# Recurrent two-layer kernel: the transpose of the maxima behind the last pair of scores, and one filler quarter per head group in a later gap

## The chip, the cores and the metric

The kernel runs on one core of a Trainium2 chip. The metric is the device time of one execution in microseconds (us). Engines: TensorE (PE; its weight loads are PEld), VectorE (DVE), ScalarE (ACT), GpSimd (POOL) and SyncE (SP, DMA issues).

## The reference

Two layers on x of shape (4, 512, 512), float32. Each is `x + s * g` on the layer norm `xn` of x.

- Layer 0, s: attention with 32 query heads and 8 key/value heads of dimension 16, rotary embedding, causal mask: `softmax(q k^T / 4 + mask) v`, then times `wo`. 4 query heads share a key/value head.
- Layer 0, g: a mixture of 8 experts, `silu` of the mean over the top 2 of `relu(xn @ W_e + b_e)`, chosen by `xn @ W_gate + b_gate`.
- Layer 1, s: a long convolution over the channel axis of 512 with a kernel from a state-space model (S4), computed from 64 complex poles, plus `D * u`.
- Layer 1, g: `silu(xn @ W^T + bias)` with a block-scaled weight.

## The kernel before, in words

Three stages follow each other on all engines: stage a (0 to about 101 us of the profile: layer norm, projections, routing), stage b (attention and experts) and stage c (from about 604 us: layer 1). Only stage b is touched.

**Stage b** has 32 head groups: 4 batches (b) times 8 key/value heads (h), each with its 4 query heads. I number them 0 to 31 (8 b + h). Each group is computed twice over. First in rows: ten score products S1 (`scores_1`, line 1562), whose masked maxima VectorE takes (`maxima`, line 1374). Then transposed: ten score products S2 (`scores_2`, lines 1588 and 1591), in which the negated row maximum enters as two more rows of the stacked operand, so that ScalarE can take the exponentials directly (`exps`, line 1485). GpSimd zeroes the masked part of the diagonal blocks (`select`, line 1308), and TensorE multiplies with the values (`values`, line 1615) in the order of key blocks 0, then 2, 3, 1.

How the maxima get there: VectorE splits them into two float32r parts (`maxima_parts`, lines 1387 and 1389), TensorE transposes them, the **turn** (`turn_maxima`, line 1599), VectorE copies the rows out (`maxima_rows`, line 1397), and SP and ACT send each one half into the operand by DMA (line 1291). ACT's DMA issue stands ahead of its last two exponentials of the group.

The stages of three groups are interleaved. While TensorE runs S2 of group g, it runs S1 of g+1, and at the end S1 products 0 and 1 of g+2. S1 has three PSUM banks: product n waits until maxima n-3 are taken; S2 likewise for the exponentials. The turn of g+1 uses the bank of S1 product 2 of g+2.

**Fillers.** Between the blocks of scores TensorE has five gaps, 0 to 4, in which it works on units of four **quarters**. A quarter is one 128x128 by 128x512 float32 product: of an expert tile (x, line 1643; the first of a unit has a bias product, line 1641) or of the output projection of a token tile (o, line 1654). `PLAN` orders the units, `SIZES` says how many quarters each gap of each group takes: SIX and EIGHT alternate, with SIX in the even groups 2 to 24, 26, 27 and 28 and EIGHT in the odd groups 3 to 25 and 29. I call these even and odd groups. All units use bank 7, so a unit's first quarter waits until ACT has read the last one (line 1495 for an expert tile).

**What follows from SIZES.** An expert tile's rows are gathered from HBM by four indirect DMAs of GpSimd (`gather`, line 1321), then transposed by VectorE (`expert_x`, line 1438), then used. `turns()` and `gathers()` compute from the gaps at which units begin and end where VectorE's transposes stand (slot 0: between the parts and the copy of the maxima; slot 1: behind the group's end) and in which of GpSimd's three slots per group the gathers stand: slot 0 behind the select of block 0, slot 1 behind that of block 2, slot 2, the last, behind those of 3 and 1. At most three gathers fit into a slot. A gather of tile m waits for the transpose of tile m-2.

At a group's end VectorE reads the values out of PSUM by a transpose (`rows_of`, line 1407: the **read**), normalises them (1412, 1416), in odd groups transposes a pair (1424), and goes on with maxima 2 to 9 of the next group. All orders are written out by hand; counts of semaphores tie the engines together.

Of the kernel before, what the change touches and what calls it, by code (L numbers as in the profile page):

```python
# [46 lines left out]
ORDER = [0, 2, 3, 1]  # L47
GAPS = 5
PLAN = "x" * 12 + ("ooxoo" + "x" * 9) * 2 + "ooxoo" + "x" * 6
SIX, EIGHT = (2, 1, 1, 1, 1), (2, 2, 1, 1, 2)  # L50
NONE = (0,) * GAPS
SIZES = [NONE, (0, 0, 0, 2, 2)] + [SIX, EIGHT] * 12 + [SIX, SIX] + [SIX, EIGHT, (2, 2, 1, 1, 0), NONE]
QUARTERS = [SIZES[KV * b:KV * (b + 1)] for b in range(NB)]
# [164 lines left out]
def build(nc, x_d, wq_d, wk_d, wv_d, wo_d, wg_d, bg_d, we_d, be_d, lam_d, p_d, q_d, vct_d, ct_d, bp_d, dd_d,  # L218
          step_d, wft_d, sc_d, bf_d, const_d, dft_d, out_d):
    ctx = ExitStack()  # L220
    with ctx:
# [532 lines left out]
        def pe_taps(e, c):  # L754

            t = nc.tensor
            if c == 0:
                e.wait_ge(s4_roots, 1)
                e.wait_ge(c_dft, 16 * 2 * KB)
                e.wait_ge(b_m, NB * NG * NJ)  # L760
            for k in range(KB):
                i = t.matmul(bank[5], roots[:, c, k:k + 1].to_broadcast([P, P]), dft[c][:, k, :],
                             start=(c + k == 0), stop=(c + k == KB))
            if c == 1:
                i.then_inc(s4_taps, 1)
# [468 lines left out]
        def next_group(b, h, n):  # L1234

            return b + (h + n) // NG, (h + n) % NG
# [382 lines left out]
        def pe_b(e):  # L1619
# [51 lines left out]
            def go(b):  # L1671
                for h in range(1 if b == 0 else 0, NG):
                    following = next_group(b, h, 1) if b * NG + h + 1 < NB * NG else None
                    after = next_group(b, h, 2) if b * NG + h + 2 < NB * NG else None
                    scores(e, (2, 3, 4), following, (0, 1, 2), (b, h))
                    quarters(b, h, 0)
                    scores(e, (5, 6, 7), following, (3, 4, 5), (b, h))
                    quarters(b, h, 1)
                    if (b, h) == (NB - 1, NG - 1):
                        pe_taps(e, 0)  # L1680
                    scores(e, (8, 9), following, (6, 7), (b, h))
                    values(e, b, h, 0)
                    quarters(b, h, 2)
                    if (b, h) == (NB - 1, NG - 1):
                        pe_taps(e, 1)
                    if following:
                        turn_maxima(e, *following)
                    scores(e, (0, 1), after, (8, 9), (b, h))
                    quarters(b, h, 3)
                    for j in ORDER[1:]:  # L1690
                        values(e, b, h, j)
                    quarters(b, h, 4)
# [461 lines left out]
```

## Time and profile before

| | us |
|---|---|
| runs | 708.52, 708.9, 706.66; median 708.52 |
| profiled execution | 706.16, span 704.4 |
| TensorE busy | 646.2 (92%) |
| VectorE busy | 560.6 (80%) |
| GpSimd, ScalarE busy | 351.3, 292.9 |
| granted TensorE clock, mean | 0.96 |
| chain that ended last | TensorE 45%, VectorE 38%, issue 7%, unknown 6% |

The profile is of one execution. The span runs from the first instruction to the last. Busy time of TensorE is modelled at the ends of matmuls. The chain goes back and forth between TensorE and VectorE, so neither alone explains the time; the waits and the timeline of single groups tell more.

### The profile page before, as it was taken

Reading aid. Unit: us, or ns where it says so; the run is one execution under the profiler, and the core shown is the slowest. Engines: PE = TensorE matmul, PEld = TensorE weight load, DVE = VectorE, ACT = ScalarE, POOL = GpSimd, SP = SyncE. Lnnn points to the kernel's source line nnn. Section 1 sums busy time; section 2 is a strip of 40 time slices with the busy share of each in tenths; the row PEclk is TensorE's granted clock in tenths of the full one; section 3 lists DMA queues with packets and bytes.
Section 4 is the critical chain, followed back from the end, with each engine's and each line's share of the span. In section 5 each row is a group of like instructions: output and inputs, shape, how many; then the busy total and the mean of one; then the engine's idle time right before and its main releaser. Section 6 shows DMA issues by size and latency. Waiting matters only on the chain.

```text
span 704.4 us, 12346 instructions
## 1 busy us (share of the span) xinstructions
PE 646.2 (92%) x3560; PEld 346.5 (49%) x3560; DVE 560.6 (80%) x1789; ACT 292.9 (42%) x535; POOL 351.3 (50%) x497
## 2 busy tenths in 40 slices
PE   8999997897899899988989999998999899999997
PEld 4888774333333334433333433343433343478886
DVE  5698998777777778887767888777987887769995
ACT  5353316333334344443434444443444443444442
POOL 3777621645454633366453346636325434656630
PEclk9999998588889999999999999999999999999999
DMA  7599979274647363372725517364353525658751
GB/s 254 153 335 277 321 181 175 45 119 137 117 138 137 85 115 56 56 121 73 118 61 96 81 34 129 85 103 86 72 105 74 144 79 208 139 113 224 197 143 74
DMA packets 55567, 92.67 MB, mean 132 GB/s; under 512 B 10328, under 2 KB 23320, under 8 KB 55504
## 3 DMA queue, kind: packets, MB, share of 16 engines
q1 hardware_dynamic: 41890, 66.45, 40.3%
q0 software_dynamic: 8576, 18.62, 12.3%
q10 hardware_dynamic: 5038, 6.84, 3.8%
q8 instruction: 29, 0.48, 0.3%
q14 instruction: 34, 0.28, 0.2%
HBM read 61.93 MB, written 29.43 MB: 130 GB/s over the span
## 4 chain that ended last, share of the span: by engine, by line
PE 45%; DVE 38%; issue 7%; another core or an unknown queue 6%; POOL 3%; DMA 1%; ACT 0%; SPq 0%; DVEq 0%; POOLq 0%; ACTq 0%
DVE bank L1374 18%; PE bank L1643 8%; PE bank L991 8%; PE bank L1562 6%; PE bank L2071 6%; PE bank L2076 4%; PE bank L1615 4%; DVE arena L1374 3%; PE bank L1654 3%; DVE arena L1438 2%; DVE arena L1407 2%; DVE m_parts L1387 2%; PE bank L1588 1%; PE bank L969 1%
## 5 line engine op out<-in xcount | busy, mean ns | idle before, releaser
L1485 ACT ACTIVATE arena<-bank 128x512 f32<-128x512 f32 x320 | 175.2, 598 | 215.3 <-PE bank L1588 159.8
L1374 DVE CUSTOM_DVE_ANT_0 bank<-bank,cst 128x384 f32<-128x384 f32 (+3 forms) x512 | 233.7, 523 | 28.0 <-PE bank L1562 21.4
L1321 POOL DMA_INDIRECT arena<-xn_rows,slots_i x156 | 148.6, 953 | 64.6 <-issue 34.0
L1308 POOL TENSOR_SCALAR_AFFINE_SELECT arena<-arena 128x512 f32<-128x512 f32 x128 | 81.9, 653 | 185.0 <-ACT arena L1485 181.3
L1643 PE MATMUL bank<-w_e,arena 128*128 x312 | 165.7, 638 | 0.0
L1562 PE MATMUL bank<-kt,qt 48*128 48x512 f32 (+1 forms) x496 | 123.9, 360 | 21.3 <-DVE arena L1374 17.7
L1562 PEld LDWEIGHTS bank<-kt,qt 48*128 48x128 f32 x496 | 77.1, 198 | 110.7 <-DVE arena L1374 65.8
L1588 PE MATMUL bank<-qt,kt 50*128 50x512 f32 x256 | 100.8, 477 | 0.9 <-ACT arena L1485 0.9
L1615 PE MATMUL bank<-arena 128*32 128x512 f32 (+3 forms) x1024 | 88.8, 462 | 0.6 <-ACT arena L1485 0.4
L1643 PEld LDWEIGHTS bank<-w_e,arena 128*128 128x128 f32 x312 | 55.0, 196 | 60.5 <-issue 56.9
L1374 DVE DVE_READ_ACCUMULATOR2_ANT arena<- 128x1 f32 x512 | 72.6, 142 | 0.0
L1407 DVE STREAM_TRANSPOSE arena<-bank 128x512 f32<-128x512 f32 x32 | 22.9, 717 | 54.9 <-remote 41.3
L1654 PE MATMUL bank<-w_proj,arena 128*128 128x512 f32 x128 | 65.0, 622 | 0.0
L825 POOL TENSOR_TENSOR s_tok<-arena 128x256 f32<-128x256 f32 (+1 forms) x64 | 33.5, 557 | 25.8 <-DVE arena L541 20.4
L991 PE MATMUL bank<-proj_high,xh 128*128 128x264 f32 (+1 forms) x128 | 45.9, 359 | 0.2 <-DVE xl L522 0.2
L1588 PEld LDWEIGHTS bank<-qt,kt 50*128 50x128 f32 x256 | 43.7, 192 | 4.4 <-ACT arena L1485 2.4
L1495 ACT ACTIVATE arena<-bank 128x512 f32<-128x512 f32 x39 | 23.4, 599 | 53.1 <-PE bank L1643 48.3
L1615 PEld LDWEIGHTS bank<-arena 128*32 128x32 f32 x1024 | 25.2, 112 | 37.5 <-issue 25.0
L991 PE MATMUL bank<-proj_low,xh 128*128 128x264 f32 (+1 forms) x128 | 43.5, 340 | 0.0
L991 PE MATMUL bank<-proj_high,xl 128*128 128x264 f32 (+1 forms) x128 | 43.2, 338 | 0.0
L1654 PEld LDWEIGHTS bank<-w_proj,arena 128*128 128x128 f32 x128 | 21.2, 189 | 26.6 <-issue 24.0
L537 DVE TENSOR_TENSOR arena<-bank,cst 128x128 f32<-128x128 f32 (+1 forms) x63 | 27.2, 476 | 6.2 <-PE bank L991 5.9
(168 smaller groups left out, 958.0 us busy)
## 6 DMA issues: line engine op xcount, KB each, us to landing
qt<-turned_parts SPq DMA_DIRECT2D x96, 128.0 KB
turned_parts<-qk_parts SPq DMA_DIRECT2D x8, 1280.0 KB
expert_rows<-arena SPq DMA_DIRECT2D x39, 256.0 KB
w_e<-in_L_ffn_W_e ACTq DMA_DIRECT2D x24, 256.0 KB, 6.2
kt<-turned_parts SPq DMA_DIRECT2D x96, 64.0 KB, 6.0
arena<-in_L_attn_x SPq DMA_DIRECT2D x16, 256.0 KB, 6.2
xn_rows<-arena SPq DMA_DIRECT2D x16, 256.0 KB, 6.0
w_e<-in_L_attn_x SPq DMA_DIRECT2D x16, 256.0 KB
```

The costliest lines, as they stand in the source:

```text
L991: i = t.matmul(out[u % 2][:, 0:n], x[:, u % 2, k, :], w[part][:, k, :], start=(k == 0 and x is xh and part == 0), stop=(k == KB - 1 and pa ...
L1308: g.affine_select(out=diag, in_=diag, compare_op=ALU.is_ge, fill=0.0, base=0, pattern=[[0, 2], [0, HALF], [1, P]], channel_multiplier=-1). ...
L1321: e.indirect_dma_start(xg[m % 2][:, n * P:(n + 1) * P], None, xn_q, bass.IndirectOffsetOnAxis(ap=slots_i[:, n, m:m + 1], axis=0)).then_inc ...
L1374: i = v.tensor_tensor_reduce(out=part, in0=part, in1=const("mask")[:, S - w:], scale=1.0, scalar=LOWEST, op0=ALU.add, op1=ALU.max, accum_o ...
L1407: v.transpose(oe.rearrange("p q c -> p (q c)"), bank[4]).then_inc(b_o, 1)
L1485: nc.scalar.activation(pt[:, s, first:second + 1:second - first].rearrange("p c r q -> p c (r q)"), s2_bank(b, h, n).rearrange("p (c x) -> ...
L1562: i = t.matmul(s1_bank(b, h, n)[:, at:at + w], stack[rows, x if r is None else r, q * P:w], kt[rows, h // 2 % 2, h % 2, 0:w], start=(x == ...
L1588: i = t.matmul(to, keys(j), queries[:, q:q + 2], start=True, stop=True)
L1615: i = nc.tensor.matmul(bank[4][VW * r:VW * (r + 1), j * P:], vb[:, j, h, :], pt[:, r // HALF, at:at + TPB - j, r % HALF, :], start=(j == O ...
L1643: i = t.matmul(bank[7], xgt[:, m % 2, k * P:(k + 1) * P], w_e[:, ex[m], k, :], start=False, stop=(k == KB - 1))
L1654: i = t.matmul(bank[to], ot[:, (b * PAIRS + k) % (PAIRS + 1), u, :], wo[:, k, :], start=(k == 0), stop=(k == KB - 1))
L2071: i = t.matmul(bank[2 + u % 2][:, :], x[:, u % 2, k, :], (w_high, w_low)[part][:, k, :], start=(k + n == 0), stop=(k + n == KB + 1))
```

## The change

It has two parts, and the schedules that are computed from `SIZES` follow.

```
-SIX, EIGHT = (2, 1, 1, 1, 1), (2, 2, 1, 1, 2)
+SIX, EIGHT = (1, 1, 1, 1, 2), (2, 1, 1, 2, 2)
```
```
                     quarters(b, h, 2)
                     if (b, h) == (NB - 1, NG - 1):
                         pe_taps(e, 1)
+                    scores(e, (0, 1), after, (8, 9), (b, h))
                     if following:
                         turn_maxima(e, *following)
-                    scores(e, (0, 1), after, (8, 9), (b, h))
                     quarters(b, h, 3)
```

TensorE's queue around the turn in group 14 (an even group), before. L1599 is the turn, L1562 and L1588 are the score products, L1641 and L1643 filler quarters, L1615 the values; b_mx is the count of VectorE's maxima parts.

```order
L1643 MATMUL bank<-w_e,arena 128x512
L1599 MATMUL bank<-cst,m_parts 32x128 [waits b_mx]
L1562 MATMUL bank<-kt,qt 128x512 [waits b_m,b_ld0]
L1588 MATMUL bank<-qt,kt 128x512 [waits b_e]
L1562 MATMUL bank<-kt,qt 128x512 [waits b_m]
L1588 MATMUL bank<-qt,kt 128x512 [waits b_e]
L1641 ISA [waits m_ye]
L1641 MATMUL bank<-be,sel_e 128x512
L1643 ISA [waits m_xt]
L1643 MATMUL bank<-w_e,arena 128x512
L1615 MATMUL bank<-arena 32x256 [waits b_sel,b_e]
```

The same place in the changed program:

```order
L1562 MATMUL bank<-kt,qt 128x512 [waits b_m,b_ld0]
L1588 MATMUL bank<-qt,kt 128x512 [waits b_e]
L1562 MATMUL bank<-kt,qt 128x512 [waits b_m]
L1588 MATMUL bank<-qt,kt 128x512 [waits b_e]
L1599 MATMUL bank<-cst,m_parts 32x128 [waits b_mx]
L1643 ISA
L1643 MATMUL bank<-w_e,arena 128x512
L1615 MATMUL bank<-arena 32x256 [waits b_sel,b_e]
L1615 MATMUL bank<-arena 32x256 x3
L1615 MATMUL bank<-arena 32x128 [waits b_sel,b_e]
```

The turn stands behind the four score products, which then no longer wait with it, and ahead of gap 3's quarter. The quarters of the units shift by one, so that another quarter of tile 18 stands there.

TensorE's queue in group 13 (an odd group), from the third S1 product of the second block to the first of the third block, that is gap 1, before:

```order
L1562 MATMUL bank<-kt,qt 128x384 [waits b_m]
L1562 MATMUL bank<-kt,qt 128x128
L1588 MATMUL bank<-qt,kt 128x512 [waits b_e]
L1643 ISA
L1643 MATMUL bank<-w_e,arena 128x512
L1624 TENSOR_LOAD eid_i
L1624 ISA x2
L1643 ISA
L1643 MATMUL bank<-w_e,arena 128x512
L1562 MATMUL bank<-kt,qt 128x256 [waits b_m]
```

And in the changed program:

```order
L1562 MATMUL bank<-kt,qt 128x384 [waits b_m]
L1562 MATMUL bank<-kt,qt 128x128
L1588 MATMUL bank<-qt,kt 128x512 [waits b_e]
L1643 ISA
L1643 MATMUL bank<-w_e,arena 128x512
L1624 TENSOR_LOAD eid_i
L1624 ISA x2
L1562 MATMUL bank<-kt,qt 128x256 [waits b_m]
```

One L1643 of gap 1 is gone from ahead of S1 product 8; it stands in gap 3, behind the turn.

GpSimd's queue in groups 8 to 11, before. L1301 begins batch 1 (group 8), each L1308 is a select (four to a group), each L1321 a gather.

```order
L1301 COPY arena<-v_tok 128x32x16
L1308 AFFINE_SELECT arena<-arena 128x2x256
L1321 DMA arena<-xn_rows,slots_i 128x128
L1308 AFFINE_SELECT arena<-arena 128x2x256 x4
L1321 DMA arena<-xn_rows,slots_i 128x128 x3
L1308 AFFINE_SELECT arena<-arena 128x2x256
L1321 DMA arena<-xn_rows,slots_i 128x128
L1308 AFFINE_SELECT arena<-arena 128x2x256 x7
L1321 DMA arena<-xn_rows,slots_i 128x128 x3
```

And in the changed program:

```order
L1301 COPY arena<-v_tok 128x32x16
L1308 AFFINE_SELECT arena<-arena 128x2x256
L1321 DMA arena<-xn_rows,slots_i 128x128
L1308 AFFINE_SELECT arena<-arena 128x2x256 x7
L1321 DMA arena<-xn_rows,slots_i 128x128 x3
L1308 AFFINE_SELECT arena<-arena 128x2x256
L1321 DMA arena<-xn_rows,slots_i 128x128
L1308 AFFINE_SELECT arena<-arena 128x2x256 x4
L1321 DMA arena<-xn_rows,slots_i 128x128 x3
```

The three gathers of tile 14 stand behind the first select of group 9 before, and behind its last one after: seven selects on are the four of group 9 with three of group 8. The same happens in groups 17 and 25. Beside this VectorE's transposes (line 1438) of tiles 12, 22, 32 go from the end of groups 8, 16, 24 to slot 0 of the group behind, those of tiles 7, 17, 27 from the end of groups 4, 12, 20 to slot 0 of 5, 13, 21, and those of tiles 8, 18, 28 from slot 0 of 5, 13, 21 to the end of these groups. ACT's and SP's reads and stores of finished units move with the gap in which the unit ends.

## Rows read from the trace of the kernel before

**Rows 1.** The page, busy time of the engines.
```profile
PE 646.2 (92%) x3560; PEld 346.5 (49%) x3560; DVE 560.6 (80%) x1789; ACT 292.9 (42%) x535; POOL 351.3 (50%) x497
```
**Rows 2.** Busy time by stretch: all groups, group 13. Columns: stretch, length, engines, clock.
```profile
134.87:573.50 438.63, 398.94 (x2197) 166.48 (x2196) 347.82 (x1258) 185.07 (x339) 217.05 (x269) 0.96 0.48 95
323.58:339.66 16.08, 14.21 (x76) 5.79 (x78) 12.28 (x43) 6.61 (x12) 10.11 (x12) 1.00 0.36 89
```
**Rows 3.** Waits: who, for whom, us in total, times, longest.
```profile
DVE arena L1407 <- remote: 41.3, 16, 3.0
...
DVE bank L1374 <- PE bank L1562: 21.4, 31, 3.2
...
PE bank L1599 <- DVE m_parts L1389: 14.7, 27, 1.6
```
**Rows 4.** Timeline of group 13: start, us, engine, line, what, idle before.
```profile
330.33 0.94 POOL L1321 DMA_INDIRECT arena<-xn_rows,slots_i  x1 [0.17 <-issue]
...
330.73 0.43 DVE L1374 CUSTOM_DVE_ANT_0 bank<-bank,cst 128x256 f32<-128x256 f32 x1 [0.65 <-PE bank L1562]
...
332.54 1.24 POOL L1308 TENSOR_SCALAR_AFFINE_SELECT arena<-arena 128x512 f32<-128x512 f32 x2
332.61 1.21 DVE L1389 SCALAR_TENSOR_TENSOR m_parts<-arena,m_parts 128x16 fp32r<-128x16 f32 x1
333.74 0.70 DVE L1438 STREAM_TRANSPOSE arena<-arena 128x512 f32<-128x512 f32 x1
...
333.88 0.28 PE L1599 MATMUL bank<-cst,m_parts 128*32 128x128 f32 x1 [0.76 <-DVE m_parts L1389]
...
335.19 0.95 POOL L1321 DMA_INDIRECT arena<-xn_rows,slots_i  x1 [1.41 <-DVE arena L1438]
...
335.37 1.08 ACT L1485 ACTIVATE arena<-bank 128x512 f32<-128x512 f32 x2 [3.03 <-PE bank L1588]
...
335.82 1.53 PE L1615 MATMUL bank<-arena 128*32 128x256 f32 x24
...
337.29 1.98 PE L1643 MATMUL bank<-w_e,arena 128*128 x4
...
337.69 0.94 POOL L1321 DMA_INDIRECT arena<-xn_rows,slots_i  x1 [0.30 <-issue]
...
339.66 0.72 DVE L1407 STREAM_TRANSPOSE arena<-bank 128x512 f32<-128x512 f32 x1 [2.78 <-remote]
```
**Rows 5.** Timeline of group 14, from the turn to the read.
```profile
348.57 0.28 PE L1599 MATMUL bank<-cst,m_parts 128*32 128x128 f32 x1 [0.31 <-DVE m_parts L1389]
...
348.79 0.72 PE L1588 MATMUL bank<-qt,kt 50*128 50x512 f32 x2
...
350.64 1.50 PE L1615 MATMUL bank<-arena 128*32 128x256 f32 x24
...
352.39 0.95 POOL L1321 DMA_INDIRECT arena<-xn_rows,slots_i  x1 [0.30 <-issue]
...
354.37 0.72 DVE L1407 STREAM_TRANSPOSE arena<-bank 128x512 f32<-128x512 f32 x1 [2.77 <-remote]
```
**Rows 6.** Timeline of groups 17 and 18: values, reads and turn.
```profile
396.29 1.50 PE L1615 MATMUL bank<-arena 128*32 128x256 f32 x24
...
397.86 0.72 DVE L1407 STREAM_TRANSPOSE arena<-bank 128x512 f32<-128x512 f32 x1 [1.25 <-PE bank L1615]
...
407.80 0.28 PE L1599 MATMUL bank<-cst,m_parts 128*32 128x128 f32 x1 [0.52 <-DVE m_parts L1389]
...
409.74 1.50 PE L1615 MATMUL bank<-arena 128*32 128x256 f32 x24
```
**Rows 7.** Timeline of TensorE's stops, and a stretch of group 15 as in rows 2.
```profile
311.39 0.44 PE L1562 MATMUL bank<-kt,qt 48*128 48x384 f32 x1 [0.99 <-DVE arena L1374]
...
357.22 0.44 PE L1562 MATMUL bank<-kt,qt 48*128 48x384 f32 x1 [1.20 <-DVE arena L1374]
...
358.54:361.95 3.41, 3.32 (x7) 1.83 (x8) 2.33 (x13) 1.08 (x2) 2.74 (x4) 0.50 0.22 58
```
**Rows 8.** Groups of instructions: line, engine, operation, count, busy, mean ns.
```profile
L1389 DVE SCALAR_TENSOR_TENSOR m_parts<-arena,m_parts 128x16 fp32r<-128x16 f32 x32 | 12.7, 398 | 1.1
```

More of the change, by code:

```diff
@@ L1685, in go @@
                         pe_taps(e, 1)
+                    scores(e, (0, 1), after, (8, 9), (b, h))
                     if following:
                         turn_maxima(e, *following)
-                    scores(e, (0, 1), after, (8, 9), (b, h))
                     quarters(b, h, 3)
```

## The prediction

> **What bounds the kernel now.** I read the page first [rows 1]: TensorE is busy 92% of the span, VectorE 80%. Then the stretch of the head groups, 134.9 to 573.5 us [rows 2]: TensorE is busy 399 of 439 us, VectorE 348. So 40 us of TensorE's time is idle there, and the question is whose waits make it. Then the table of waits [rows 3]: TensorE waits 14.7 us in 27 places for VectorE's negated maxima before the turn (line 1599), and VectorE waits 41.3 us in 16 places before it reads the values out of PSUM (line 1407), with the releaser "remote", which is none that the trace can name.
>
> The timeline of group 13 shows what that is [rows 4]. The last values end at 335.82 + 1.53 = 337.35, but VectorE starts to read them at 339.66, 2.3 us late. In between GpSimd issues three gathers, 1.25 apart, the last from 337.69 to 338.63, and VectorE goes on 1.0 behind its end. Group 14 repeats it [rows 5]: values end 352.14, the last gather ends 353.34, the read starts 354.37. Where no gather stands there the read follows at once: values end 397.79, read 397.86 [rows 6]. I take it that TensorE's counts reach the others late while gathers are issued. All 16 "remote" places have three gathers in GpSimd's last slot of the group, and of the groups in steady running that have them only 20 and 21 escape.
>
> So there are two kinds of cycle. **Held groups**: the turn, VectorE's transpose of an expert tile (0.70), three gathers, one microsecond, the read: 339.66 - 333.88 = 5.78, and 5.80 in group 14, whatever TensorE does between; then VectorE's own chain from the read to the next turn, 348.57 - 339.66 = 8.91 in group 14, 16.08 - 5.78 = 10.30 in group 13 [rows 2, 4, 5]. VectorE and GpSimd bound them. **Free groups**: values end 3.44 behind the turn, and the chain from read to turn takes 9.94 [rows 6]; TensorE and VectorE are nearly level.
>
> **The change part by part.**
>
> *The turn behind the last score pair.* The four score products take 0.72 [rows 5]. They now fill TensorE's wait, at most 14.7 in 27 places, mean 0.54. But the turn starts when line 1389 ends (333.82, turn 333.88), before and after: nothing on VectorE becomes earlier. What follows it (the copy of the rows, two DMA issues, the last two exponentials) ends at 336.45, 2.57 behind the turn [rows 4], and the last values need it. Today the values start 1.94 behind the turn; in an even group they could start 0.7 sooner, but their last part still waits for the exponentials, so their end stays. Value 0 of a possible 0 to -14.7; I take 0, since the row nearest, the exponentials' end, doesn't move. On TensorE's queue the scores, the quarters and the values stand behind the turn's wait as before, the one score pair no longer. The new place also moves the turn behind the wait for the next stacks' loads; these were issued more than a group (14 us) earlier, so I add nothing.
>
> *The quarter out of gap 1 in odd groups.* A quarter costs 0.96 (two take 1.98 with the last one's tail [rows 4]). In group 13 VectorE stands 0.65 before 330.73, waiting for the scores behind the two quarters. With one quarter these come 0.96 earlier and the wait is gone. Eight odd groups (3, 5, 7, 13, 15, 21, 23, 29) have it at 0.65 to 0.9: 8 x 0.7 = -5.6. Bounds: 0, if the counts are then held by the gather at 330.33, and -7. In even groups the quarter leaves gap 0, where VectorE doesn't wait if the read was held: 0. Group 2: -0.5.
>
> *The quarters added behind.* In odd groups one more in gap 3 makes the values start at +2.1 instead of +1.94; held groups don't feel it. In free odd groups (9, 11, 17, 19, 25) TensorE reaches the turn later by the scores' 0.72 less its present wait (0.2 to 0.76): +0.3 each, and the same in 27 and 30: +2.1. Bounds 0 and +5.
>
> *Expert tiles and gathers that move along.* The schedule derives them. Three transposes (0.70) leave VectorE's chain from read to turn in groups 5, 13, 21 and three enter it in 6, 14, 22: 0 within 0.3. In 9, 17, 25 the gathers of tiles 14, 24, 34 move from the group's head to its last slot. These groups are free now and become held: the cycle of the group behind goes from 13.45 (411.24 - 397.79, values to values [rows 6]) to 14.79 (352.14 - 337.35 [rows 4, 5]): 3 x 1.3 = +3.9, bounds 0 and +4.2.
>
> *The stall of line 1389.* In group 13 it takes 1.21 and ends with the two selects that started before it (332.54, 1.24 together [rows 4]); its mean over 32 is 0.40 [rows 8]. The selects here stand behind two gathers (the first at 330.33), so they don't move up, while VectorE arrives 0.7 earlier and can pass before them. In 5, 13 and 21 fewer gathers are ahead, the selects move too, and part of the stall stays. Over seven held odd groups I take 7 x -0.3 = -2.1. Bounds: -0.8 x 4 for the four with a full stall (1.21 down to the mean) and +0.8 x 3 for those without, if they get one.
> The Trainium skill (SBUF — State Buffer, section "Who interferes with whom") states that a VectorE instruction with two SBUF inputs and a GpSimd instruction that reads SBUF exclude each other, whoever issues first holding for its whole length. The 1.21 beside the 1.24 agrees. By that rule passing or not passing a select is all or nothing, and the term would be -3 or +2 rather than between.
>
> *Clock.* In group 15 TensorE stood 1.20 before 357.22; from 358.54 to 361.95 the granted clock is 0.50, 1.2 GHz [rows 7], which takes 1.7 of its time. The mean clock of 0.96 over 438.6 [rows 2] is 17.5 us of it, 6 in the first 12 us, the rest in groups 3, 4, 15, 20 and 21; I reckon that 8 of it is on the path. Odd groups lose this stop (a quarter more stands ahead of it). Even groups reach their second block of scores 0.96 earlier, less 0.2 for the later values, and wait there for the maxima: group 12's stop, 0.99 before 311.39 [rows 7], becomes 1.75, others 1.2 to 1.6. I take -1, bounds -5 and +6.
> The Trainium skill (TensorE: Matmul & The Clock Gate, Part 1) says that the throttled clock is the default and activity releases it. That speaks against the change, which gathers idle time into fewer, longer stops. The trace agrees in one place, 1.20 and then 0.50.
>
> **Sum.** -5.6 - 0.5 + 2.1 + 0 + 3.9 - 2.1 - 1.0 = -3.2. The profiled execution took 706.16 (span 704.4 and 1.8 around it); it would be 703.0. The median of the runs shown is 708.52, 2.4 above it, so against the median the forecast is 705.3; I say 705.2. A measurement of this kernel can tell about 0.3%, 2.1 us, from no change: below 706.4 is faster, above 710.6 slower.
>
> **Rivals.**
> *Nothing is left of it* (0.22). The 5.78 of the held groups doesn't move; if the scores' counts are held by the gather in gap 1 too, -5.6 halves and the stall stays: about 708.5. For it: the gather at 330.33 lies right there. Against it: VectorE's wait at 330.73 ended while that gather ran.
> *Clock: slower* (0.18). Thirteen even groups run behind a held read once 9, 17 and 25 are held too. If the stop at their second block lets the clock fall each time, the half-speed stretch (3.41) adds 1.7 of TensorE's work, of which VectorE's slack covers 0.6: 13 x 1.1 = 14.3 instead of the 7 left in the sum. That is +7 on the forecast: 712.3. It decides from about six such falls on. For it: group 15 did it at 1.20. Against it: group 12's 0.99 passed without.
> *TensorE is the bound after all* (0.12). Then the 14.7 comes off whole, less the +3.9 and +2.1 that remain and a few us for gaps whose quarter was needed: about -10, 698.5. For it: 92% busy. Against it: 5.78 and 5.80 in rows 4 and 5, with two quarters behind the values in one and one in the other.
> *The forecast* (0.48), own range 702 to 708.
>
> **Range and chances.** 700.5 to 711 leaves out the far half of the TensorE rival and the bad end of the clock one. Faster: three quarters of the forecast's 0.48, the TensorE rival's 0.12, 0.03 of the first rival: 0.51. Slower: 0.17 from the clock and 0.03 from the rest: 0.20. Same: 0.29.
>
> **What would show it.** The turn's wait (14.7) is small, but "remote" waits before line 1407 stand in 19 places instead of 16, with groups 9, 17 and 25 among them and reads 5.8 behind the turn there. VectorE's waits for line 1562 fall from 21.4 to about 14. The chain from read to turn is 8.2 to 9.5 in groups 13 and 15. The clock is below 1 in some even groups' second block; if it falls in more than six, I am on the wrong side. If reads no longer follow the gathers' end by 1.0, the picture of the held counts is wrong.

## The result, and the profile after

| | before | after |
|---|---|---|
| median of 7 runs, us | 708.9 (706.66 to 710.03) | 715.62 (711.6 to 720.61) |
| ratio, 95% interval | | 1.0103 (1.0071 to 1.0135) |
| profiled execution, us | 706.16, span 704.4 | 720.61, span 718.8 |
| granted clock, mean of that execution | 0.960 | 0.940 |

The change costs 1%. The forecast was 705.2 with a range up to 711, so it has the wrong sign. The profiled execution is the longest of its seven, so its sums are somewhat large; where that matters I use a second trace, or the clock and span of every run.

The page of the kernel after, busy times and granted clock in 40 slices:

```profile
PE 655.7 (91%) x3560; PEld 348.2 (48%) x3560; DVE 553.6 (77%) x1789; ACT 290.9 (40%) x535; POOL 352.6 (49%) x497
PEclk9999997589899999989999899989989998999999
```

Against [rows 1], TensorE is busy 9.5 us longer with the same instructions: the clock row has an 8 every few slices. Its waits (engine, line, releaser: us in total, times, longest), to be held against [rows 3]:

```profile
DVE arena L1407 <- remote: 44.1, 16, 3.8
DVE arena L1397 <- PE bank L1599: 22.5, 19, 3.3
DVE bank L1374 <- PE bank L1562: 16.9, 25, 1.3
PE bank L1615 <- ACT arena L1485: 14.0, 18, 2.2
PE bank L1599 <- DVE m_parts L1389: 2.1, 2, 1.4
```

TensorE's wait before the turn is gone (14.7, now 2.1), as forecast, and so is part of VectorE's wait for scores (21.4, now 16.9). In their place VectorE waits 22.5 us for the turn (4.5 before, a row that I had not looked at), and TensorE waits 14.0 for the last exponentials before the last values (0.4 before). Group 16 (the turn at 380.34) shows both:

```profile
378.12 1.13 PE L1654 MATMUL bank<-w_proj,arena 128*128 128x512 f32 x2
378.96 0.55 DVE L1389 SCALAR_TENSOR_TENSOR m_parts<-arena,m_parts 128x16 fp32r<-128x16 f32 x1
379.68 0.50 PE L1562 MATMUL bank<-kt,qt 48*128 48x512 f32 x1 [0.43 <-DMA qt<-turned_parts]
380.34 0.28 PE L1599 MATMUL bank<-cst,m_parts 128*32 128x128 f32 x1
380.66 0.28 DVE L1397 COPY arena<-bank 32x128 f32<-32x128 f32 x1 [1.15 <-PE bank L1599]
381.41 0.86 PE L1615 MATMUL bank<-arena 128*32 128x256 f32 x16
382.83 0.85 PE L1615 MATMUL bank<-arena 128*32 128x384 f32 x8 [0.56 <-ACT arena L1485]
```

Line 1389 ends at 379.51, TensorE's filler at 379.25. In the old order the turn would have started at about 379.57, since it follows line 1389 by 0.06 there. Now the first score product waits 0.43 for the load of its stack, the four products take 0.66, and the turn starts 0.83 behind line 1389. The values then start 1.07 behind the turn (1.94 before) and stop 0.56 for the exponentials, which hang on the turn as before.

Group 17, one of the three that were to become held:

```profile
396.29 1.50 PE L1615 MATMUL bank<-arena 128*32 128x256 f32 x24
397.49 0.95 POOL L1321 DMA_INDIRECT arena<-xn_rows,slots_i  x1 [0.30 <-issue]
399.50 0.72 DVE L1407 STREAM_TRANSPOSE arena<-bank 128x512 f32<-128x512 f32 x1 [3.79 <-remote]
```

Values end 397.79, the last gather 398.44, the read starts 1.06 later, 5.75 behind the turn. That step held.

The clock, in the group that follows (TensorE's rows, then the stretch's clock: us, busy times, PEclk):

```profile
402.41 0.44 PE L1562 MATMUL bank<-kt,qt 48*128 48x384 f32 x1 [0.76 <-DVE arena L1374]
404.54 2.07 PE L1654 MATMUL bank<-w_proj,arena 128*128 128x512 f32 x2
```
```profile
403.87:410.69 6.82, 6.82 (x23) 2.57 (x23) 4.63 (x22) 2.04 (x4) 1.87 (x3) 0.50 0.48 81
```

TensorE stops 0.76 before the second block, and from 403.87 to 410.69 it has 0.50, 1.2 GHz; two quarters take 2.07 instead of 1.13. Such stretches between 148 and 600 us sum to 27.3 us in the first trace of before (17.1 and 20.5 in two later ones) and 47.8 in that of after; in a second trace of after (below) to 41.0. There eight of them lie in even groups, 8, 10, 12, 16, 18, 20, 24 and 28, and each of the eight stands behind a stop of 0.80 to 1.87 us before the second block of its group; two stops as long before a filler, 1.86 and 1.90 us in groups 6 and 14 of the same trace, have none behind them. Three of the eight:

```profile
254.54:257.95 3.41, 3.41 (x14) 1.42 (x18) 2.47 (x15) 1.94 (x4) 0.64 (x1) 0.50 0.93 151
285.26:288.67 3.41, 3.41 (x18) 1.21 (x17) 3.13 (x16) 1.08 (x2) 1.63 (x3) 0.50 0.58 117
...
558.33:561.74 3.41, 3.41 (x14) 1.42 (x18) 2.46 (x15) 1.34 (x3) 0.64 (x1) 0.50 0.98 203
```

### The profile page after: what moved, and what is told of

Same layout as the page of the kernel before. It is cut to its first block, busy times and chain, and to the rows that moved or that the text cites. A ratio compares the mean times of both kernels' runs of the same rounds, so it can differ in the third digit from the quotient of the medians.

```text
span 718.8 us, 12346 instructions
## 1 busy us (share of the span) xinstructions
PE 655.7 (91%) x3560; PEld 348.2 (48%) x3560; DVE 553.6 (77%) x1789; ACT 290.9 (40%) x535; POOL 352.6 (49%) x497
## 4 chain that ended last, share of the span: by engine, by line
PE 53%; DVE 23%; issue 7%; another core or an unknown queue 5%; DMA 4%; POOL 3%; ACT 2%; SPq 1%; ACTq 1%; DVEq 0%; POOLq 0%
DVE bank L1374 9%; PE bank L1643 9%; PE bank L1562 7%; PE bank L991 7%; PE bank L1615 6%; PE bank L2071 5%; PE bank L1654 5%; PE bank L2076 4%; PE bank L1588 2%; DMA arena<-xn_rows,slots_i 2%; DVE arena L1374 1%; ACT arena L1485 1%; DVE arena L1407 1%; POOL w_e L1840 1%
## 5 line engine op out<-in xcount | busy, mean ns | idle before, releaser
L1374 DVE CUSTOM_DVE_ANT_0 bank<-bank,cst 128x384 f32<-128x384 f32 (+3 forms) x512 | 233.0, 521 | 22.0 <-PE bank L1562 16.9
L1308 POOL TENSOR_SCALAR_AFFINE_SELECT arena<-arena 128x512 f32<-128x512 f32 x128 | 83.6, 666 | 201.7 <-ACT arena L1485 198.6
L1321 POOL DMA_INDIRECT arena<-xn_rows,slots_i x156 | 148.9, 955 | 61.1 <-issue 33.6
L1643 PE MATMUL bank<-w_e,arena 128*128 x312 | 165.8, 639 | 5.1 <-DVE arena L1438 4.6
L1562 PE MATMUL bank<-kt,qt 48*128 48x512 f32 (+1 forms) x496 | 125.7, 367 | 20.3 <-DVE arena L1374 17.6
L1562 PEld LDWEIGHTS bank<-kt,qt 48*128 48x128 f32 x496 | 78.9, 205 | 131.9 <-DVE arena L1374 74.5
L1615 PE MATMUL bank<-arena 128*32 128x512 f32 (+3 forms) x1024 | 95.5, 476 | 16.2 <-ACT arena L1485 14.0
L1588 PE MATMUL bank<-qt,kt 50*128 50x512 f32 x256 | 100.3, 479 | 0.9 <-ACT arena L1485 0.9
L1643 PEld LDWEIGHTS bank<-w_e,arena 128*128 128x128 f32 x312 | 54.9, 197 | 57.8 <-issue 53.9
L1654 PE MATMUL bank<-w_proj,arena 128*128 128x512 f32 x128 | 67.5, 641 | 0.9 <-ACT s_tok L1476 0.9
L1615 PEld LDWEIGHTS bank<-arena 128*32 128x32 f32 x1024 | 24.5, 112 | 56.5 <-issue 24.9
L1588 PEld LDWEIGHTS bank<-qt,kt 50*128 50x128 f32 x256 | 44.2, 194 | 5.0 <-ACT arena L1485 2.4
L825 POOL TENSOR_TENSOR s_tok<-arena 128x256 f32<-128x256 f32 (+1 forms) x64 | 33.5, 556 | 25.9 <-DVE arena L541 20.5
L991 PE MATMUL bank<-proj_high,xl 128*128 128x264 f32 (+1 forms) x128 | 43.2, 338 | 0.0
L1654 PEld LDWEIGHTS bank<-w_proj,arena 128*128 128x128 f32 x128 | 21.9, 197 | 29.6 <-issue 23.9
L537 DVE TENSOR_TENSOR arena<-bank,cst 128x128 f32<-128x128 f32 (+1 forms) x63 | 27.3, 476 | 6.3 <-PE bank L991 6.0
```

Of the source, the lines that this page charges most:

```text
L825: i = g.tensor_tensor(o[:, :, :, c, :], xc[:, :, :, c, :], xs[:, :, :, 1 - c, :], op)
L991: i = t.matmul(out[u % 2][:, 0:n], x[:, u % 2, k, :], w[part][:, k, :], start=(k == 0 and x is xh and part == 0), stop=(k == KB - 1 and pa ...
L1308: g.affine_select(out=diag, in_=diag, compare_op=ALU.is_ge, fill=0.0, base=0, pattern=[[0, 2], [0, HALF], [1, P]], channel_multiplier=-1). ...
L1321: e.indirect_dma_start(xg[m % 2][:, n * P:(n + 1) * P], None, xn_q, bass.IndirectOffsetOnAxis(ap=slots_i[:, n, m:m + 1], axis=0)).then_inc ...
L1374: i = v.tensor_tensor_reduce(out=part, in0=part, in1=const("mask")[:, S - w:], scale=1.0, scalar=LOWEST, op0=ALU.add, op1=ALU.max, accum_o ...
L1562: i = t.matmul(s1_bank(b, h, n)[:, at:at + w], stack[rows, x if r is None else r, q * P:w], kt[rows, h // 2 % 2, h % 2, 0:w], start=(x == ...
```

## The experiments

They ran in five sets, each on a chip of its own with runs of before beside them. The chips turned out to be of two kinds (in these sets no chip served twice, so it isn't shown that the chip and not the session makes the difference). On the first kind before takes 704 to 707 us (708.9 on the chip of the record) and VectorE's reads are held, as in the prediction. On the second before takes 670 and no read is held. I call them **held chips** and **free chips**.

Two sums serve for reading. Of each run, the **clock loss** is its span times (1 - granted clock), and the **rest** is the span without it. The 13 runs of after on two held chips scatter around a line of 0.93 us of span for 1 us of clock loss (correlation 0.88), so most of it is on the path. Of each trace, the periods of groups 3 to 29 (values' end to values' end) are split at four points: **lag** (values' end to read), **chain** (read to the end of line 1389), **late** (from there to the turn), **values** (turn to values' end).

| run | change against before | chip | median | ratio (95%) | clock loss | rest |
|---|---|---|---|---|---|---|
| c1_after | all | held | 717.38 | 1.0206 (1.0164 to 1.0248) | +14.5 | -0.9 |
| f1_order | turn behind the pair | held | 711.55 | 1.0121 (1.0084 to 1.0158) | +3.5 | +3.4 |
| f2_sizes | new SIX and EIGHT | held | 706.99 | 1.0047 (1.0022 to 1.0072) | +4.1 | -0.4 |
| g1_odd | new EIGHT | held | 703.7 | 0.9958 (0.9937 to 0.9979) | +2.1 | -5.3 |
| e5_split | turn between S2 and S1 pair | held | 707.24 | 1.0029 (1.0001 to 1.0057) | +2.0 | +0.4 |
| e6_order_loads | turn behind the pair, loads on ACT | held | 719.22 | 1.0208 (1.0176 to 1.024) | +8.5 | +5.5 |
| f3_gathers2 | two gathers in last slot | held | 695.07 | 0.9886 (0.9852 to 0.992) | -2.0 | -6.9 |
| g2_odd_gathers2 | new EIGHT, two gathers in last slot | held | 700.45 | 0.9913 (0.988 to 0.9946) | +0.5 | -7.8 |
| e1, d1 | turn behind the pair | free | 679.72, 681.2 | 1.0138, 1.0144 | +0.5, -0.2 | +8.7, +10.1 |
| e2, d2 | new SIX and EIGHT | free | 680.32, 681.05 | 1.0156, 1.0151 | +2.4, +0.9 | +7.6, +9.2 |
| e3_order_odd | turn behind the pair, new EIGHT | free | 676.17 | 1.0099 (1.006 to 1.0139) | +2.5 | +3.8 |
| e4_odd | new EIGHT | free | 675.66 | 1.0077 (1.0045 to 1.0109) | +1.9 | +3.4 |
| e7_fill | all, a quarter twice | free | 686.93 | 1.0256 (1.0209 to 1.0303) | -0.6 | +17.6 |
| e8_gathers2 | two gathers in last slot | free | 678.91 | 1.0116 (1.0074 to 1.0159) | +1.2 | +6.3 |

The last two columns are differences of means, with 95% intervals of about 1.4 to 2.9 us either way for the clock loss and 1.1 to 2.8 for the rest. The intervals of the doubled ratios are 1.0094 to 1.0183, 1.0092 to 1.0196, 1.0119 to 1.0194 and 1.0109 to 1.0194.

Sums of one trace each, groups 3 to 29, us:

| trace | periods | lag | chain | late | values |
|---|---|---|---|---|---|
| before, mean of three (held) | 406.5 | 42.3 | 267.2 | 1.8 | 95.2 |
| after, mean of two (held) | 418.1 | 35.1 | 261.9 | 17.9 | 103.3 |
| f1_order | 404.6 | 37.6 | 264.0 | 12.2 | 90.9 |
| f2_sizes | 414.7 | 37.4 | 258.2 | 6.1 | 113.1 |
| g1_odd | 402.8 | 38.4 | 255.8 | 2.0 | 106.4 |
| e5_split | 408.8 | 43.7 | 266.4 | 7.1 | 91.6 |
| f3_gathers2 | 391.3 | 14.2 | 262.3 | 1.6 | 113.3 |
| e1_order (free) | 381.1 | 5.3 | 265.2 | 19.0 | 91.4 |

The traces of f1 and f2 are of their shortest and longest execution (705.39 and 713.25), 6 off the medians on either side; I take from them where time stands, and how much from the medians. The three traces of before differ by up to 6 us in the chain (264.3 to 270.2), so smaller differences there say little.

The late term has two sources, which the traces tell apart: the filler in front of the score products can itself end behind line 1389, or the products, 0.60 us from the filler's end to the turn, push the turn. In f1_order fillers that end late make up 1.4 us of the 12.2 and waits for loads 0.5; the rest, about 10, is the products. In the two traces of after late fillers make up 7.4 and 5.9 us, most of it in groups with a half-speed stretch; there too some 10 us are left for the products.

**First set, a free chip.** The parts one by one:

```
e1: the new order, SIX, EIGHT = (2, 1, 1, 1, 1), (2, 2, 1, 1, 2)
e2: the old order, SIX, EIGHT = (1, 1, 1, 1, 2), (2, 1, 1, 2, 2)
e3: the new order, SIX, EIGHT = (2, 1, 1, 1, 1), (2, 1, 1, 2, 2)
e4: the old order, SIX, EIGHT = (2, 1, 1, 1, 1), (2, 1, 1, 2, 2)
```

> The new place of the turn alone, old SIZES. Median of before 708.9, of the changed kernel 715.6. Theory CLOCK (the quarter that leaves gap 0 of the even groups makes TensorE stop before the second block, the clock falls to 1.2 GHz there, and the half-speed stretches cost the 7 us): the stops stay as in before, at most 7 half-speed stretches in stage b, 706 to 709. Rival TURN LATE (the four score products stand ahead of the turn, which starts 0.4 to 0.8 behind line 1389's end in some twelve even groups and in the odd ones too, and all that follows moves): 713 to 716, with no more half-speed stretches than before. Rival HELD READS (groups 9, 17, 25 and the moved transposes): no effect here, within 0.3% of before.

> The new SIZES alone, turn in its old place. CLOCK: stops before the second block in the even groups and half-speed stretches as in the changed kernel (about 54 us of them in stage b against 27 before), 713 to 716. TURN LATE: the turn is not late, 703 to 707. HELD READS: about +4 on before, 712 to 714, with reads held in 9, 17 and 25 and half-speed stretches as before.

> The new place of the turn and the odd groups' new EIGHT; the even groups keep SIX of before, with two quarters in gap 0. CLOCK: the stops before the second block stay under 1.2, few half-speed stretches, odd groups shorter, 703 to 707. TURN LATE: 711 to 715. HELD READS: 711 to 713.

> The odd groups' new EIGHT alone: turn in its old place, SIX of before. CLOCK: 702 to 706, faster than before, since only the odd groups' wait at the third block goes. TURN LATE: the same, 702 to 706. HELD READS: 710 to 713, since this kernel has the gathers of tiles 14, 24 and 34 in the last slot of 9, 17 and 25 too.

Each part alone costs time here, and mostly not by the clock, as the rest shows. In e1 the turn is late by 19.0 us in sum. In e2 and e4 it isn't (1.8 and 1.5), but the values take 117.6 and 116.0 us against 91.4 in e1, with another quarter ahead of them in the odd groups. One wait of e1 and one place (group 16):

```profile
PE bank L1562 <- DMA qt<-turned_parts: 8.0, 10, 2.2
```
```profile
360.22 0.17 DVE L1389 SCALAR_TENSOR_TENSOR m_parts<-arena,m_parts 128x16 fp32r<-128x16 f32 x1
361.16 0.50 PE L1562 MATMUL bank<-kt,qt 48*128 48x512 f32 x1 [1.23 <-DMA qt<-turned_parts]
361.82 0.28 PE L1599 MATMUL bank<-cst,m_parts 128*32 128x128 f32 x1
```

The turn stands behind a product that waits for a DMA, and is 1.43 late. I had added nothing for this wait. No read is held. In e1's group 14 all three gathers of the last slot are issued, the last until 337.02, and VectorE reads at 336.84, 0.13 behind the values (335.86 + 0.85); there is no remote wait in the trace:

```profile
335.86 0.85 PE L1615 MATMUL bank<-arena 128*32 128x384 f32 x8 [0.35 <-ACT arena L1485]
336.08 0.94 POOL L1321 DMA_INDIRECT arena<-xn_rows,slots_i  x1 [0.30 <-issue]
336.84 0.72 DVE L1407 STREAM_TRANSPOSE arena<-bank 128x512 f32<-128x512 f32 x1 [0.82 <-PE bank L1615]
```

**Second set, a held chip.** Before and after again, and two orders:

> The kernel before once more, unchanged: its trace on the chip of this call. In the four kernels run so far on another chip (before 669.99 there, not 708) VectorE's read follows the values at once, though GpSimd issues the same three gathers. If the held reads belong to the chip (theory), the trace has no remote waits before line 1407 and all groups take 13.4 to 14.6 where before takes about 670, and has the 41 us of them where before takes about 708. If they came from the changed orders (rival), this trace has them in either case.

c0_before: 704.43, ratio 0.9999 (0.9971 to 1.0026), 43.2 us of remote waits in 16 places. The held reads are not of the changed orders: the unchanged kernel has them here.

> The changed kernel once more, unchanged, beside before on the same chip. Where before takes about 670: theory TURN LATE adds to e1 (ratio 1.0138) and e2 (1.0156) for 1.025 or more if the two parts cost in different places, and about 1.015 if both push the same wait. Where before takes about 708: 1.010 as measured first.

1.0206: larger than the first 1.0103, with intervals that don't meet. Both say slower; what sets the difference between the chips is open. Here all of the loss is clock loss, 40.0 us a run against 25.5, and the rest is 0.9 less than that of before. On the chip of the record after has 37.8 a run; of before only the profiled execution's clock is known, 28.2, so there it is about +10.

```
e5:
+                    scores(e, (), None, (8, 9), (b, h))
                     if following:
                         turn_maxima(e, *following)
-                    scores(e, (0, 1), after, (8, 9), (b, h))
+                    scores(e, (0, 1), after, (), None)
```

> Old SIZES. The S2 pair (8, 9) goes ahead of the turn, the S1 pair (0, 1) stays behind it. Theory LOADS (in e1 TensorE waits in 10 places, 8.0 us, before S1 product 0 for the DMA of the stacks, which now delays the turn behind it): e1's loss mostly goes, ratio 0.997 to 1.005, and the turn starts within 0.1 of line 1389's end. Rival WORK AHEAD (what delays the turn is the 0.72 of products itself, TensorE being full): half of it stays, ratio 1.006 to 1.010.

1.0029. With the S1 pair behind the turn, three quarters of the order's loss (1.0121 on another held chip, below) are gone. That is in LOADS' range, but its mechanism doesn't stand behind it on a held chip: TensorE waits only 0.5 us for loads before S1 products in f1, and the turn here is still 7.1 us late in sum (12.2 in f1), not within 0.1 each time. With half of the products ahead of the turn about half of the added lateness is left, as WORK AHEAD said, though less than half of the lost time.

```
e6 (on e1):
-                        load_stacks(e, *next_group(b, h, 3))
+                        load_stacks(e, *next_group(b, h, 3), (0,))
 and at the end of ACT's odd groups:
+                        load_stacks(e, *next_group(b, h, 3), (1,))
```

> The new place of the turn with old SIZES (as e1), and ACT issues half of each stack load (six of the twelve DMAs) at the end of the odd groups, so that the load lands some 3 us earlier. LOADS: the waits of line 1562 for the DMA into qt go (8.0 us in 10 places in e1) and the ratio falls from e1's 1.0138 to 1.000 to 1.004. WORK AHEAD: 1.008 to 1.014.

The waits for the load are gone, but the kernel is as slow as after. ACT's copy of a finished unit (line 1495) now stands behind the six issues, and TensorE waits for it (line 1645 is 1643 here):

```profile
371.64 0.60 ACT L1495 ACTIVATE arena<-bank 128x512 f32<-128x512 f32 x1 [2.53 <-issue]
372.61 3.58 PE L1645 MATMUL bank<-w_e,arena 128*128 x4 [2.59 <-ACT arena L1495]
```

The edit has brought a stop of its own (9.0 us in 5 places), so the time tells nothing between the two theories. The trace does: without a wait for loads the turn is still late by 10.4 us in sum.

**Third set, a free chip.** d1 and d2 are e1 and e2 again:

> The new place of the turn alone, old SIZES (the kernel of e1), for a chip on which the reads are held (before about 705). There c1_after lost 2.06% (14.5 us) and its half-speed stretches inside the head groups went from about 5 to 11. WORK AHEAD (the S1 pair ahead of the turn makes the turn and all behind it later by up to 0.72): in held groups VectorE's maxima decide and TensorE has time, so ratio 1.000 to 1.005. CLOCK (the values start at +1.07 behind the turn, stop for the last exponentials, the cycle gets a second stop, and the clock falls): 1.008 to 1.015, with more than 8 half-speed stretches in the groups.

> The new SIZES alone (the kernel of e2) on a chip with held reads. CLOCK by the quarter missing in gap 0 of even groups: stops of 1.2 to 1.9 before the second block, 9 or more half-speed stretches, ratio 1.008 to 1.015. HELD READS in groups 9, 17 and 25 alone: 3 x 1.0 to 1.7 = +3 to +5, less the 4 to 6 of the odd groups' shorter chains: 0.997 to 1.002 and about as many half-speed stretches as before.

They repeat the first set, and say nothing of a held chip.

```
e7 (on after), for the even groups' gap 0 (the same for quarters of the output projection):
+                if twice:
+                    t.matmul(bank[7], xgt[:, m % 2, k * P:(k + 1) * P], w_e[:, ex[m], k, :], start=False, stop=False)
```

> The changed kernel, with the one quarter of gap 0 of the even groups (2 to 24, 26 to 28) computed twice: 16 more quarters, 15 us more work for TensorE, placed where it stood still before the second block; its outputs are not the reference's. CLOCK: the stop before the second block goes and with it most half-speed stretches there; ratio 1.003 to 1.010 against the 1.0206 of c1_after. Rival TENSORE IS THE BOUND: the 15 us come on top, 1.03 to 1.04. If the stops matter but not the clock: 1.018 to 1.022.

1.0256. The edit adds a quarter in 15 groups (the expectation counted 16). No after ran beside it, and on a free chip the clock loss is that of before anyway (-0.6). The clock was not tested.

> The kernel before, but at most two gathers in GpSimd's last slot of a group; the third moves to the first slot of the next group. Theory HELD BY GATHERS (VectorE's read follows the end of the last gather of the slot by 1.0): the last gather ends 1.25 earlier, so the reads of 16 groups follow their values by 1.0 to 1.2 instead of 2.3, and VectorE's remote waits fall from 41 to about 20; 8 to 18 us faster, ratio 0.975 to 0.989. Rival BURST ELSEWHERE (the gather that moves holds the counts at the next group's head as well, where VectorE waits for S1 products): 0.995 to 1.005. On a chip without held reads: 0.997 to 1.003.

1.0116, above the 1.003 expected: where nothing is held, moving a gather only costs. What it costs by was not looked into.

**Fourth set, a held chip.** The parts again (f1 is the kernel of e1, f2 that of e2), and the gathers (f3 is the kernel of e8):

> The kernel before, unchanged, for its trace on this chip. If before takes about 670 here, as on two chips so far, the trace has no remote waits before line 1407, groups 9 to 29 take 13.4 to 13.8 each in pairs of 27.2, and GpSimd's gathers stand and last as on the other chips: then the held reads are of the chip. If about 705, remote waits of 40 to 44 us in 14 to 17 places as in c0_before.

704.04, ratio 1.0002 (0.9973 to 1.003), 44.8 us of remote waits in 17 places.

> The new place of the turn alone, with old SIZES, on the next chip. Twice 1.014 where before takes 670 (10 us in 30 groups, the even groups' turn 0.5 to 1.4 behind line 1389's end). Where before takes 705: WORK AHEAD gives 1.000 to 1.005, since in a held group only VectorE's chain counts; CLOCK gives 1.008 to 1.015 with more than 8 half-speed stretches in the groups.

1.0121, half clock loss (+3.5) and half rest (+3.4). The turn is late by 12.2 us in sum, of which about 10 are the products. Group 15 shows one place without any wait:

```profile
361.97 1.13 PE L1643 MATMUL bank<-w_e,arena 128*128 x2
362.71 0.17 DVE L1389 SCALAR_TENSOR_TENSOR m_parts<-arena,m_parts 128x16 fp32r<-128x16 f32 x1
363.02 0.49 PE L1562 MATMUL bank<-kt,qt 48*128 48x512 f32 x1
363.70 0.28 PE L1599 MATMUL bank<-cst,m_parts 128*32 128x128 f32 x1
```

Line 1389 ends at 362.88, the filler at 363.10, and the turn starts 0.60 behind the filler, 0.82 behind line 1389. So WORK AHEAD has the mechanism, but as I had bounded it (1.005) it is too small, and CLOCK's more than eight stretches are not there either (six, 23.9 us, in its shortest execution).

> The new SIZES alone on the next chip. Twice 1.015 where before takes 670 (odd groups 14.0 to 14.7 instead of about 13.7, because in the free running the quarter moved into gap 3 stands ahead of the values). Where before takes 705: CLOCK by gap 0 gives 1.008 to 1.015 and 9 or more half-speed stretches; held reads in 9, 17 and 25 alone give 0.997 to 1.002.

1.0047: between the two theories, clock loss +4.1 and the rest -0.4. So separately the parts add 3.5 and 4.1 of clock loss, together 14.5 on another held chip and about 10 on the chip of the record. The ratios themselves do about add up: 1.0121 and 1.0047 give 1.0168, between the 1.0103 and the 1.0206 of after. One place where the traces differ in the stops alone is 360 to 425 us, groups 15 to 19. There f2 has one stop of TensorE of over 0.55 us (0.80), f1 has four of 0.56, and neither has a half-speed stretch. In after there are both kinds (1.21, 0.56, 0.76, 0.56), and behind the 0.76 the clock falls. First f2, then f1, then after:

```profile
360.00:425.00 65.00, 60.57 (x353) 25.59 (x360) 52.75 (x203) 29.51 (x54) 28.85 (x38) 1.00 0.41 73
```
```profile
360.00:425.00 65.00, 60.55 (x354) 24.76 (x357) 51.08 (x192) 28.12 (x52) 28.10 (x36) 1.00 0.43 74
```
```profile
360.00:425.00 65.00, 60.49 (x329) 24.71 (x328) 49.06 (x191) 27.05 (x51) 25.76 (x34) 0.95 0.39 67
```

The 0.56 are the new stop before the last values, which the order brings. The 1.21 and 0.76 of after are those before the second block, where the quarter of gap 0 is missing; f2, which misses it too, has none there in this stretch, and its 0.80 stands before the turn. It is one stretch of one trace each: that the two kinds of stop together make the clock fall is suggested by it, not shown.

```
f3:
-            at[(*divmod(g, KV), slot)], waiting = waiting[:3], waiting[3:]
+            n = 2 if slot == 2 else 3
+            at[(*divmod(g, KV), slot)], waiting = waiting[:n], waiting[n:]
```

> The kernel before with at most two gathers in GpSimd's last slot. 1.0116 where before takes 670 and no read is held. Where before takes 705: HELD BY GATHERS gives reads 1.0 to 1.2 behind the values instead of 2.3, remote waits of about 20 instead of 41 us, and 0.975 to 0.995 (the 8 us that it costs on the other chips taken off the gain); BURST ELSEWHERE gives 1.005 to 1.015 with as many us of remote waits as before.

0.9886, faster than both kernels. The lag falls from 42.3 to 14.2 us, as HELD BY GATHERS said. But the values' part grows by 18 (95.2 to 113.3), and the remote waits of f3 tell where it went (its lines are one higher: 1398 is the copy of the turned maxima, 1408 the read, 1486 the exponentials):

```profile
DVE arena L1398 <- remote: 16.2, 10, 2.1
ACT arena L1486 <- remote: 12.7, 7, 3.5
DVE arena L1408 <- remote: 2.1, 1, 2.1
```

Group 15 shows one:

```profile
356.10 0.28 PE L1600 MATMUL bank<-cst,m_parts 128*32 128x128 f32 x1
356.14 0.94 POOL L1322 DMA_INDIRECT arena<-xn_rows,slots_i  x1 [0.31 <-ACT arena L1486]
358.20 0.28 DVE L1398 COPY arena<-bank 32x128 f32<-32x128 f32 x1 [1.54 <-remote]
```

The moved gather now stands beside the turn, and the copy goes on 1.12 behind its end (357.08). So other counts of TensorE's can be held by a gather too, not only that of the values. Not every one is: in [rows 4] VectorE went on at 330.73, in the middle of the gather of 330.33. Both theories were partly right.

**Fifth set, a held chip.** g1 is the kernel of e4, and g2 has the edit of f3 besides.

> The odd groups' new EIGHT alone (the kernel of e4, 1.0077 where before takes 670), turn and SIX as before. Where before takes 705: if the loss of the new SIZES (f2, 1.0047, 37 us of half-speed stretches in the groups against 17 to 27 before) comes from the quarter missing in gap 0 of the even groups (CLOCK), this one has the stretches of before and is 0.988 to 0.997, since the chain from read to maxima parts gets 8 to 9 us shorter over groups 3 to 29 and the three newly held groups give back 4. If it comes from EIGHT itself (values later behind the two quarters of gap 3, three more held reads), 1.001 to 1.006.

0.9958, 3.0 us faster than before; the rest is 5.3 less. The forecast for the odd groups' terms was -3.8 (-5.6 + 3.9 - 2.1), so their total is about right. By the trace that is in part luck: the chain is 11.4 shorter against the 7.7 forecast, lag and values together 7.3 longer against 3.9. With f2's 1.0047 the new SIX costs about 0.9% (two chips); on the free chip of the first set e2 and e4 differ by 0.8% as well. Most of it is not clock: the rests differ by 4.9 and 4.2 us, the clock losses by 2.0 and 0.5. Where in the groups it arises was not followed further.

> The same with at most two gathers in GpSimd's last slot. Where before takes 705: f3 gave 0.9886 for the two gathers alone; with EIGHT, under CLOCK 0.978 to 0.986, under EIGHT ITSELF 0.988 to 0.994, the best kernel of the study in either case if the two gains add. Where before takes 670: 1.012 to 1.020.

0.9913: no better than f3 (0.9886, on another chip). The gains don't add. The values' part is 125.5 us in its trace against 95.2 of before, and ScalarE's exponentials alone have 21.4 us of remote waits in 12 places.

## Why the prediction was wrong, point by point

- **The turn, value 0, "the turn starts when line 1389 ends, before and after".** This is the step that failed most. It was true of before, where the sum of the late term is 1.8 us. In f1, the order alone, it is 12.2, about 10 of it by the four products; in after it is 17.9, with late fillers beside that. The row that I read it from (turn 0.06 behind line 1389) was one where TensorE was waiting 0.76; group 14 beside it had 0.31 [rows 5]. The mean wait was 0.54, and the products that I moved ahead of the turn take 0.60 of queue time. In the three traces of before the filler ends 0.6 or more ahead of line 1389 in only 7, 3 and 3 of 27 groups. An estimate from these traces, 0.60 less the head start of each group, gives 7, 9 and 10 us of lateness, near what f1 showed. I had priced it at +2.1, in the free odd groups (and 27 and 30) only; 11 and 19, which I named among these, are not free, their reads follow the turn by 5.8. The order alone measured 1.0121, about +8.5.
- **"The new place also moves the turn behind the wait for the next stacks' loads; ... I add nothing."** Failed too. The last of the twelve loads is issued some 7 us ahead, not 14 (group 16: its last ones begin at 372.15 and 372.61, the wait ends at 379.68). On a free chip that wait is 8.0 us of the 19.0 by which the turn is late. On held chips it is small (0.4 in after, 0.5 in f1), and the products decide.
- **"Their end stays" for the values.** Right for the order: 3.34 behind the turn in group 16. What I didn't draw from it is that the 0.87 by which the values start sooner becomes a stop of TensorE. The new EIGHT does move their end (the values' part is 106.4 in g1, 95.2 before), mostly where the read is held anyway.
- **Quarter out of gap 1 (-5.6) and the stall of line 1389 (-2.1).** The sign was right: the chain is 5.3 shorter in after and 11.4 in g1, where it is part of a total of -3.0 us. The stall itself did not move: line 1389 takes 12.7, 12.6 and 12.6 us in the traces of before and 13.4 and 11.6 in those of after. So the rule of the Trainium skill (SBUF — State Buffer, "Who interferes with whom"), by which this term would be -3 or +2, decided nothing here: the sums moved by -1 to +1.
- **Even groups' quarter out of gap 0, value 0.** Failed: the new SIX costs about 0.9% (f2 against g1), most of it not by the clock.
- **Held groups 9, 17, 25 (+3.9).** Held as forecast, with reads 5.7 to 5.8 behind the turn. The lag is 7 us shorter in all though. I take it that values that end later run into gathers that don't move with them: in g1 the turn is on time, yet the odd groups' values end 0.8 to 0.9 later and their lag is shorter by as much.
- **Clock, -1 with bounds to +6.** Failed in size and sign: +14.5 on the second held chip, about +10 on the record's. My rival "clock: slower" (712.3, chance 0.18) fits the second trace, with eight falls in even groups against its "about six", each behind a stop before the second block. But it let the missing quarter do it alone, and the new sizes alone (f2) give +4.1, of which the new EIGHT alone (g1) already has +2.1 (2 to 3 us either way). The order's stop before the values was in none of my terms; the order alone adds +3.5. Why both together add more is not shown.
- **The sum.** Without the +2.1 of the late turn, the terms of the new sizes were -5.3; f2 measured +3.3. With f1's +8.5 the parts come to +11.8, and by its ratios after measured +7.3 and +14.5. One rival's sum doesn't come out: -14.7 + 3.9 + 2.1 is -8.7 before the "few us" that make it smaller, not -10.

The record of what the profile was to show: the turn's wait small, right; remote waits in 16 places instead of 19, wrong in number, with the three named among them; VectorE's wait for line 1562 at 16.9, near the 14; the chain from read to turn 9.4 and 9.3 in group 13, right, and 9.5 and 10.2 in group 15, at the edge and beyond it; the clock below 1 in more than six even groups, "I am on the wrong side".

Open: why order and SIZES cost 1.0103 on one held chip and 1.0206 on another, how the clock loss divides between the two kinds of stop, and where the new SIX costs its 4 to 5 us. A fill of the stop on a held chip was not tried.

## What to carry to other kernels

Before you move work into a wait, compare the work with the wait group by group, not with the place where the wait is longest, and ask what the moved work waits for itself: what stands behind it gets that wait too. Look at two parts of a change together where both make the same engine stop; here they cost 10 to 14.5 us of clock loss together and 7.6 apart, though on different chips, so this is a hint and no proof. For each run take span times (1 - granted clock) off the span first. What is left is a first division between schedule and clock.

## What the runs showed of the hardware that I had not expected

- The same program takes 704 to 709 us on some chips (four) and 670 on others (two), and the difference is mostly not the clock: without the clock loss 676 to 679 against 651. On the 670 chips the gathers take as long (0.95 us each), but no count of TensorE's is held by them: the eight traces taken there have no "remote" wait.
- On the other chips a count of TensorE's that falls into a gather can be seen late, by VectorE 1.0 to 1.1 us behind the end of the last gather in a row (1.06 at line 1407, 1.12 at line 1397). ScalarE (line 1485) has such remote waits too, 12.7 us in 7 places in f3. Not every count is held: VectorE went on at 330.73 in [rows 4], inside a gather. And group 20 of before escapes because its gathers stand elsewhere in time: the values end at 441.79, between a gather that ends at 440.57 and the next at 442.86, and the read follows by 0.12.
- A stop of 0.76 us in TensorE was followed by a half-speed stretch in after (group 18), while the 1.21 of group 16 in the same trace was not, nor were four stops of 0.56 in f1 or one of 0.80 in f2 in the same 65 us.
